# Layer 0's combining stage: gate, product and the first slots ahead of the preparation of attention's weights

## The chip, the cores and the metric

One core of a Trainium2 chip runs the whole program. The time is device microseconds of one execution; runs of one kernel are compared by their median. The engines are PE (TensorE), DVE (VectorE), ACT (ScalarE), POOL (GpSimd) and SP (SyncE, which issues DMAs).

## The reference, cut to what matters

A macaron block over 4096 tokens of width 256: half a mixture-of-experts layer, attention, half a mixture-of-experts layer, all in float32.

```python
def ffn(x, Wg, W1, W2, W3, Ws1, Ws2, Ws3):           # T = 4096, E = 32, TOP_K = 4
    weights, indices = top_k(softmax(x @ Wg), 4)
    y = zeros_like(x)
    for e in range(E):                                 # routed tokens of one expert
        y = y.at[tok].add(swiglu(x[tok], W1[e], W2[e], W3[e]) * w[:, None])
    return y + swiglu(x, Ws1, Ws2, Ws3)                # shared expert, for all tokens

def attn(x, qkv_w, qkv_b, proj_w, proj_b):             # 16 heads of width 16
    q, k, v = split(x @ qkv_w.T + qkv_b)
    return softmax(q @ k.T / sqrt(16)) @ v @ proj_w.T + proj_b

x = x + 0.5 * ffn(layernorm(x), ...)
x = x + attn(layernorm(x), ...)
x = x + 0.5 * ffn(layernorm(x), ...)                   # the same weights again
```

## The kernel before

The program runs in stages with a barrier between them: routing, experts, combining (`combine_project`), attention, and then routing, experts and combining again. The change is in `combine_project` alone, which runs once, at 387.9 to 608 us.

This stage handles 32 tiles of 128 tokens (`NT`), in 8 blocks of 4 (`TPB`). For each tile it fetches the four rows that the experts wrote for each token, one indirect DMA for each of the four (`pair_d` to `Y`), and adds them to `X` with their weights. It adds half of the shared expert's output, measures mean and variance, normalises, turns the block by matmuls with the identity, and multiplies by attention's weights to give q, k and v.

Before the tiles come two preparations. The first is the shared expert for block 0: `up` (matmuls into `psA` and `psB`), `gated` (Silu, ACT), `hidden` (gate times `psB`, DVE), for two halves `m`. The second is attention's weights: ACT squares four row blocks of `raw` and sums them, DVE's `balance_weights` works out powers of two from the sums (12 tiny operations) and scales the four row blocks, PE turns all eight row blocks through `psQ[0]` and `psQ[1]`, ACT copies them out, and v's bias is folded into `out_bias` (a matmul into `psV`, an addition on DVE).

The order on each engine is written out by hand, as a loop over slots `s` = 0 to 39. In slot `s` DVE adds tile `s` (`gathered`, four operations; `hidden` in odd slots; `shared`; `measured`), PE does a fourth of `up` for the next block and `down` for tile `s`, and from slot 7 on (`LAG`) PE also does `value` and `query_key` for a tile seven earlier. `down(t)` waits until DVE's `shared(t - 1)` has read `psZ`. At the last slot of a block DVE prepares the variance, in the slot behind it ACT takes the root and DVE normalises.

POOL issues the 128 gathers in a row, each with a small memset behind it (`pause`) that waits for the gather's issue. There are 16 slots in `Y`, so gather 17 (tile 4) waits for DVE's `gathered(0)`, and generally tile `t` for `gathered(t - 4)`; no weight of attention stands in that queue.

Of the kernel before, what the change touches and what calls it, by code (L numbers as in the profile page):

```python
# [28 lines left out]
HSC = HS // P  # L29
# [920 lines left out]
def combine_project(nc, a, f_sem, sb, pb, X, XNT, pair_d, pair_slot, pair_weight, ws1, ws3, ws2, ident, env):  # L950
# [6 lines left out]
    QB = 3  # L957
    LAG = TPB + 3
    SLOTS = NT + LAG + 1
    y_in = [env["sem"](f"y_in{s}") for s in range(YS)]  # L960
    sem = env["heads_sem"]
    V, ops, spare, norms = env["V"], env["ops"], env["spare"], env["norms"]
# [18 lines left out]
    with ExitStack() as c:  # L981
# [37 lines left out]
        with nc.Block() as block:  # L1019
# [66 lines left out]
            def _(pe):  # L1086
# [12 lines left out]
                def down(t):  # L1099
                    b, u = t // TPB, t % TPB  # L1100
                    if u == 0:
                        pe.wait_ge(f_sem("s_hid"), (b + 1) * HSC)
                    if t >= 1:
                        pe.wait_ge(f_sem("z_added"), t)
                    for m in range(HSC):
                        last = pe.matmul(psZ[:, :], hid[:, b % 2, m, u * P:(u + 1) * P], ws2[:, m, :],
                                         start=(m == 0), stop=(m == HSC - 1))
                    last.then_inc(f_sem("z_ready"), 1)

                def turn(b, pair):  # L1110
# [5 lines left out]
                            last = pe.transpose(psT[:, u, c, :], xn[:, 2 * pair + u, c * P:(c + 1) * P], ident[:, :])  # L1116
                    last.then_inc(sem("turned"), 1)

                def value(b, u):
                    t = b * TPB + u  # L1120
                    pe.wait_ge(sem("xnt_ready"), 2 * b + u // 2 + 1)
                    if t >= 1:
                        pe.wait_ge(sem("v_out"), t)
                    for c in range(DC):
                        last = pe.matmul(psV[:, :], xnt[:, c, u * P:(u + 1) * P], wt[:, c, 2 * D:],
                                         start=(c == 0), stop=(c == DC - 1))
                    last.then_inc(sem("v_in"), 1)
# [24 lines left out]
                pe.wait_ge(f_sem("ws"), 48)  # L1152
                for piece in range(2 * HSC):
                    up(0, piece)
                pe.wait_ge(sem("raw"), 32)
                for n, b in enumerate(ORDER):
                    if b < NE:
                        pe.wait_ge(sem("w_scaled"), b + 1)
                    if n >= 2:
                        pe.wait_ge(sem("w_out"), n - 1)  # L1160
                    for c in range(DC):
                        last = pe.transpose(psQ[n % 2][:, c * P:(c + 1) * P], raw[:, b, c * P:(c + 1) * P], ident[:, :])
                    last.then_inc(sem("w_turned"), 1)
                pe.wait_ge(sem("w_out"), NW)
                pe.wait_ge(sem("vwide"), 1)
                for c in range(DC):
                    last = pe.matmul(psV[:, :], vwide[:, c, :], pwt[:, c, :], start=(c == 0), stop=(c == DC - 1))
                last.then_inc(sem("vb_in"), 1)
                pe.wait_ge(sem("out_bias"), 1)
                pe.wait_ge(sem("heads"), 3)  # L1170
                for s in range(SLOTS):
                    now, past = projecting(s), projecting(s - TPB)
                    if s // TPB + 1 < NB:
                        up(s // TPB + 1, s % TPB)
                    if s < NT:
                        down(s)
                    if now is not None and now[1] == 0:
                        turn(now[0], 1)
                    if past is not None and past[1] == 0:
                        measure(past[0])  # L1180
# [14 lines left out]
            def _(act):  # L1195
                def gated(b, m):
                    act.wait_ge(f_sem("s_up"), b * 2 * HSC + 2 * m + 1)
                    if b * HSC + m >= 1:
                        act.wait_ge(f_sem("s_hid"), b * HSC + m)
                    act.activation(gate[:, :], psA[:, :], ACT.Silu).then_inc(f_sem("s_gate"), 1)  # L1200
# [19 lines left out]
                def squared(b, e):  # L1220
                    act.wait_ge(sem("high"), b * NE + e + 1)
                    act.activation(square[:, e, :], parts[:, e, 0, :], ACT.Square).then_inc(sem("squared"), 1)

                act.wait_ge(sem("raw"), 32)
                for e in range(NE):
                    act.activation(raw_sq, raw[:, e, :], ACT.Square, accum_out=square_sum[:, e:e + 1])\
                       .then_inc(sem("w_squared"), 1)
                    act.wait_ge(sem("w_squared"), e + 1)
                for m in range(HSC):
                    gated(0, m)  # L1230
                for n, b in enumerate(ORDER):
                    act.wait_ge(sem("w_turned"), n + 1)
                    dst = wt[:, :, b * P:(b + 1) * P] if b < NQ else pwt[:, :, (b - NQ) * P:(b - NQ + 1) * P]
                    act.activation(dst, psQ[n % 2][:, 0:D].rearrange("p (c q) -> p c q", c=DC), ACT.Copy).then_inc(sem("w_out"), 1)
                for s in range(SLOTS):
                    now, past = projecting(s), projecting(s - TPB)
                    if s % TPB == 0 and 1 <= s // TPB <= NB:
                        b = s // TPB - 1
                        act.wait_ge(sem("var"), b + 1)
                        act.activation(dev[:, b * TPB:(b + 1) * TPB], var[:, b * TPB:(b + 1) * TPB], ACT.Sqrt).then_inc(sem("dev"), 1)  # L1240
                    if now is not None and now[1] == 0:
                        turned(now[0], 1)
                    if past is not None and past[1] == 0:
                        b = past[0]
                        act.wait_ge(sem("norm_out"), 2 * b + 1)
                        if b == 0:
                            act.wait_ge(sem("steps_out"), 16 * 4)
                        act.activation(norms[:, b * BLK:(b + 1) * BLK], psQ[output(b, NE) % QB][0:NH, :], ACT.Copy)\
                           .then_inc(sem("norm_kept"), 1)
                    if s // TPB + 1 < NB and s % 2 == 0:  # L1250
                        gated(s // TPB + 1, s % TPB // 2)
                    if now is not None:
# [28 lines left out]
            def _(v):  # L1281
# [52 lines left out]
                    v.wait_ge(sem("norm_kept"), b + 1)  # L1334
                    v.sem_inc(sem("q_out"), 2)

                v.wait_ge(sem("bias"), 16)
                v.wait_ge(sem("w_squared"), NE)
                balance_weights(v, own.link, raw, bias, square_sum, span, expo_i, expo_f, power, sem("w_scaled"))
                v.wait_ge(sem("vbias"), 16)  # L1340
                v.tensor_copy(vwide, vbias[:, :].unsqueeze(2).to_broadcast([P, DC, P])).then_inc(sem("vwide"), 1)
                for m in range(HSC):
                    hidden(0, m)
                v.wait_ge(sem("pbias"), 16)
                v.wait_ge(sem("vb_in"), 1)
                v.tensor_tensor(out_bias[:, :], psV[:, :], out_bias[:, :], ALU.add).then_inc(sem("out_bias"), 1)
                for s in range(SLOTS):
                    now, past = projecting(s), projecting(s - TPB)
                    if s < NT:
                        gathered(s)  # L1350
                        if s % 2 == 1 and s // TPB + 1 < NB:
                            hidden(s // TPB + 1, s % TPB // 2)
                        shared(s)
                        measured(s)
                    if s < NT and s % TPB == TPB - 1:
# [461 lines left out]
```

## Time and profile before

| | us |
|---|---|
| median of 3 runs | 2913.71 (2913.23 to 2915.76) |
| the profiled execution | 2915.8 |
| its span | 2914.1 |
| busy in the span: PE, DVE, ACT, POOL | 2646.3, 2242.2, 2198.4, 715.6 |

The stage takes 220 of the 2914 us. Attention, which follows it, takes most of the span and is not touched. A row of a timeline reads: start, duration, engine, line, operation, what it writes <- what it reads, shapes, count, and in brackets how long the engine had been idle before it and what ended that. Rows in sequence of one line are merged. A float32 matmul of the program stands as two matmul instructions on PE.

### The profile page before, as it was taken

The page shows a single profiled execution, that of the slowest core. Times are in us where ns is not written, and L with a number is a line of the kernel's source. Part 1 is how long each engine was busy: PE and PEld are TensorE (multiplying, and loading weights), DVE is VectorE, ACT ScalarE, POOL GpSimd, SP SyncE. Part 2 cuts the span into 40 slices and gives each one's busy share as a digit, 9 for nine tenths or more (in the row PEclk, how much of TensorE's full clock was granted, in tenths as well). Part 3 has the DMA queues.
Part 4 walks back from the last instruction along what each step waited for, and adds up shares of the span by engine and source line. Part 5 has one row for each costly group of instructions (what it writes and reads, how often), then busy time and mean ns, then how long its engine had stood idle before and what let it go on. Part 6 is the DMA issues. An engine that isn't in the chain of part 4 may idle for free. (4 is left out here: it accounts for less than half of the span.)

```text
span 2914.1 us, 54682 instructions
## 1 busy us (share of the span) xinstructions
PE 2646.3 (91%) x17803; PEld 1087.4 (37%) x17803; DVE 2242.2 (77%) x4357; ACT 2198.4 (75%) x3178; POOL 715.6 (25%) x1002
## 2 busy tenths in 40 slices
PE   5799979959999999999999999999999984999971
PEld 5499845511222222122121222222222162999541
DVE  6777758858888888888888888888888767777454
ACT  4644425559999999999999999999999945444320
POOL 1566668730000000000000000000000014666576
PEclk9999999979999999999999999999999985999985
DMA  6555655520010010010010010010000026555644
GB/s 185 153 170 171 160 119 140 140 57 3 5 25 3 5 25 3 5 25 4 4 25 5 3 25 5 3 25 5 3 10 27 3 90 191 166 171 164 116 125 121
DMA packets 132280, 195.63 MB, mean 67 GB/s; under 512 B 22534, under 2 KB 99526, under 8 KB 130662
## 3 DMA queue, kind: packets, MB, share of 16 engines
q1 hardware_dynamic: 104208, 116.85, 14.3%
q0 software_dynamic: 27648, 75.53, 10.7%
q8 instruction: 146, 2.39, 0.4%
q14 instruction: 86, 0.70, 0.1%
q10 hardware_dynamic: 192, 0.15, 0.0%
HBM read 124.80 MB, written 67.50 MB: 66 GB/s over the span
## 5 line engine op out<-in xcount | busy, mean ns | idle before, releaser
L1686 ACT ACTIVATE RB<-psS 128x1024 f32<-128x1024 f32 x1856 | 1702.4, 1338 | 17.5 <-PE psS L1609 17.4
L1651 PE MATMUL psO<-RB,values 128*32 128x512 f32 x7424 | 991.8, 606 | 0.1
L1609 PE MATMUL psS<-WE 51*128 51x512 f16 x3712 | 667.4, 386 | 38.2 <-SPq L1574 8.1
L1609 PEld LDWEIGHTS psS<-WE 51*128 51x128 f16 x3712 | 165.1, 93 | 1034.7 <-ACT RB L1686 1013.0
L1707 DVE TENSOR_SCALAR scaled<-psO 128x512 int32<-128x512 f32 x384 | 265.0, 690 | 173.2 <-PE psO L1609 166.1
L660 POOL DMA_INDIRECT xg<-xn_d,index x320 | 305.3, 954 | 185.3 <-issue 152.1
L686 PE MATMUL psH<-xgt,chosen 128*128 128x128 f32 x2560 | 341.4, 277 | 0.0
L1568 POOL COPY values<-WE 128x464 f32<-128x464 f32 x12 | 6.8, 568 | 1266.4 <-PE psO L1651 1266.4
L686 PEld LDWEIGHTS psH<-xgt,chosen 128*128 128x128 f32 x2560 | 314.3, 193 | 0.6 <-issue 0.2
L773 ACT ACTIVATE gate<-psH 128x128 f32<-128x128 f32 x320 | 88.7, 277 | 261.5 <-PE psH L686 255.1
L1651 PEld LDWEIGHTS psO<-RB,values 128*32 128x32 f32 x7424 | 146.3, 108 | 308.1 <-issue 291.2
L695 PE MATMUL psO<-WE,hid 128*128 x640 | 191.0, 381 | 0.6 <-ACT ob L777 0.6
L749 DVE TENSOR_TENSOR hid<-gate,psH 128x128 f32<-128x128 f32 x320 | 92.0, 287 | 121.2 <-ACT gate L773 120.5
L777 ACT ACTIVATE ob<-psO 128x256 f32<-128x256 f32 x320 | 122.8, 384 | 52.6 <-PE psO L695 46.4
L736 DVE COPY chosen<-WE 128x512 f32 x320 | 134.9, 422 | 30.3 <-issue 27.9
L1609 PE MATMUL psO<-WE 51*128 51x512 f16 x384 | 145.6, 379 | 12.5 <-DVE scaled L1707 12.5
L676 PE MATMUL psX<-ident,xg 128*128 128x128 f32 x640 | 125.9, 279 | 22.2 <-DMA xg<-xn_d,index 21.0
L743 DVE COPY xgt<-psX 128x256 f32<-128x256 f32 x320 | 133.3, 417 | 13.3 <-PE psX L676 12.6
L1718 DVE TENSOR_SCALAR scaled<-scaled 128x1024 int32<-128x1024 int32 x192 | 135.9, 708 | 0.0
L1078 POOL DMA_INDIRECT WE<-pair_d,pair_slot x128 | 126.0, 985 | 24.7 <-issue 20.9
L1723 DVE SCALAR_TENSOR_TENSOR WE<-series 128x1024 f32<-128x1024 f32 x96 | 112.9, 1217 | 0.0
L1738 DVE SCALAR_TENSOR_TENSOR WE<-WE,scaled 128x1024 f32<-128x1024 f32 x96 | 112.9, 1217 | 0.0
(245 smaller groups left out, 3161.7 us busy)
## 6 DMA issues: line engine op xcount, KB each, us to landing
pair_d<-ob SPq DMA_DIRECT2D x320, 128.0 KB, 2.1
WE<-part_d SPq DMA_DIRECT2D x84, 128.0 KB
xn_d<-ws SPq DMA_DIRECT2D x64, 128.0 KB, 1.7
WE<-in_W SPq DMA_DIRECT2D x2, 4096.0 KB, 24.0
part_d<-raw SPq DMA_DIRECT2D x32, 256.0 KB, 3.0
xg<-xn_d,index POOLq DMA_INDIRECT x320
RA<-in_x SPq DMA_DIRECT2D x8, 512.0 KB, 7.3
head_d<-sums SPq DMA_DIRECT2D x128, 32.0 KB, 1.8
```

What stands on the lines that cost most here:

```text
L660: pool.indirect_dma_start(xg[:, u, :], None, xn_d, bass.IndirectOffsetOnAxis(ap=index[:, w, u:u + 1], axis=0))\
L676: last = pe.transpose(psX[j % 2][:, c * P:(c + 1) * P], xg[:, j % U, c * P:(c + 1) * P], ident[:, :])
L686: last = pe.matmul(psH[j % 2][:, n * P:(n + 1) * P], chosen[:, j % 2, c, n, :], xgt[:, j % 2, c * P:(c + 1) * P], start=(c == 0), stop=(c ...
L695: pe.matmul(psO[j % 2][:, :], hid[:, j % U, :], WE[:, e, DC * 2 * H:], start=True, stop=True).then_inc(sem("down"), 1)
L736: v.tensor_copy(chosen[:, j % 2, :, :, :].rearrange("p c n h -> p (c n h)"), WE[:, e, 0:DC * 2 * H])\
L743: v.tensor_copy(xgt[:, j % 2, :], psX[j % 2][:, :]).then_inc(sem("xgt_ready"), 1)
L1078: pool.indirect_dma_start(Y[:, s, :], None, pair_d, bass.IndirectOffsetOnAxis(ap=pair_slot[:, t, k:k + 1], axis=0))\
L1609: return pe.matmul(ps, K[r][rows, kt * P:(kt + 1) * P], Q[r][rows, first:first + BLK], start=True, stop=True)
L1651: last = pe.matmul(psO[g % 2][32 * j:32 * (j + 1), :], values[:, r, j % 2, kt, :], weights, start=(kt == 0), stop=(kt == order(g)[-1]))
L1686: act.activation(probs[m % RING], psS[m % HELD][:, :], ACT.Exp, scale=SCALE).then_inc(sem("exped"), 1)
L1707: v.tensor_scalar(scaled[at(g, u)][:, n * BLK:(n + 1) * BLK], bank[:, :], SCALE * LOG2E * 2 ** 23, LOWEST, ALU.mult, ALU.max).then_inc(sem ...
L1718: v.tensor_scalar(scaled[k], scaled[k], EXPONENT, FLIP, ALU.bitwise_and, ALU.bitwise_xor)\
```

## The change

`up(0, ...)` stays first on PE. Everything else of the weights' preparation moves back:

- ACT: `gated(0, 0)` and `gated(0, 1)` now stand ahead of the four squares; the eight copies out of `psQ` move into slot 3.
- DVE: `hidden(0, 0)`, `hidden(0, 1)` and slot 0 now stand ahead of `balance_weights` and the copy of v's bias; the addition to `out_bias` moves to slot 3, behind `measured(3)` and ahead of the variance.
- PE: the 16 transposes and the two matmuls of v's bias move to slot 3, behind `down(3)`. The wait for `out_bias` moves from slot 0 to the first `value`.

The instructions themselves, the DMAs and POOL's and SP's queues stay as they were.

```diff
+    WEIGHTS_AT = 3
 # PE
+                def weights():
+                    pe.wait_ge(sem("raw"), 32)
+                    for n, b in enumerate(ORDER):
+                        if b < NE:
+                            pe.wait_ge(sem("w_scaled"), b + 1)
+                        if n >= 2:
+                            pe.wait_ge(sem("w_out"), n - 1)
+                        for c in range(DC):
+                            last = pe.transpose(...)
+                        last.then_inc(sem("w_turned"), 1)
+                    pe.wait_ge(sem("w_out"), NW)
+                    pe.wait_ge(sem("vwide"), 1)
+                    ...                                # matmuls into psV
+                    last.then_inc(sem("vb_in"), 1)
 def value(b, u):
+                    if t == 0:
+                        pe.wait_ge(sem("out_bias"), 1)
...
                 for piece in range(2 * HSC):
                     up(0, piece)
-                pe.wait_ge(sem("raw"), 32)
-                ...                                    # the same as in weights()
-                pe.wait_ge(sem("out_bias"), 1)
                 pe.wait_ge(sem("heads"), 3)
                 for s in range(SLOTS):
...
                     if s < NT:
                         down(s)
+                    if s == WEIGHTS_AT:
+                        weights()
 # ACT
+                for m in range(HSC):
+                    gated(0, m)
                 act.wait_ge(sem("raw"), 32)
                 for e in range(NE):
                     act.activation(raw_sq, raw[:, e, :], ACT.Square, ...)
-                for m in range(HSC):
-                    gated(0, m)
-                for n, b in enumerate(ORDER):
-                    ...                                # eight copies
...
+                    if s == WEIGHTS_AT:
+                        for n, e in enumerate(ORDER):
+                            ...                        # the same eight copies
 # DVE
-                v.wait_ge(sem("bias"), 16)
-                v.wait_ge(sem("w_squared"), NE)
-                balance_weights(...)
-                v.wait_ge(sem("vbias"), 16)
-                v.tensor_copy(vwide, ...)
                 for m in range(HSC):
                     hidden(0, m)
-                v.wait_ge(sem("pbias"), 16)
-                v.wait_ge(sem("vb_in"), 1)
-                v.tensor_tensor(out_bias[:, :], psV[:, :], out_bias[:, :], ALU.add)
                 for s in range(SLOTS):
...
                         measured(s)
+                    if s == 0:
+                        ...                            # balance_weights and the copy, with their waits
+                    if s == WEIGHTS_AT:
+                        ...                            # the addition to out_bias, with its waits
```

On DVE at the stage's start, before (`span`, `expo` and `power` belong to `balance_weights`, `shid` is `hidden`, RA is `X`; L1341 is the copy of v's bias and L1346 the addition to `out_bias`):

```order
L945 TENSOR_TENSOR bias<-bias,power 128x4 [waits a_dve]
L947 TENSOR_SCALAR raw<-raw,power 128x256 [waits a_dve]
L947 TENSOR_SCALAR raw<-raw,power 128x256 x3
L1341 COPY axn<-vbias 128x256 [waits a_vbias]
L1287 TENSOR_TENSOR shid<-sgate,psB 128x512 [waits f0_s_up,f0_s_gate] x2
L1346 TENSOR_TENSOR WE<-psV,WE 128x256 [waits a_vb_in,a_pbias]
L1293 SCALAR_TENSOR_TENSOR RA<-WE,pair_weight,RA 128x256 [waits k_y_in0]
```

and there now:

```order
L1295 TENSOR_TENSOR shid<-sgate,psB 128x512 [waits f0_s_up,f0_s_gate] x2
L1301 SCALAR_TENSOR_TENSOR RA<-WE,pair_weight,RA 128x256 [waits k_y_in0]
L1301 SCALAR_TENSOR_TENSOR RA<-WE,pair_weight,RA 128x256 [waits k_y_in1,f0_y_used]
L1301 SCALAR_TENSOR_TENSOR RA<-WE,pair_weight,RA 128x256 [waits k_y_in2,f0_y_used]
L1301 SCALAR_TENSOR_TENSOR RA<-WE,pair_weight,RA 128x256 [waits k_y_in3,f0_y_used]
L1307 SCALAR_TENSOR_TENSOR RA<-psZ,RA 128x256 [waits f0_z_ready,f0_y_used]
L1312 BN_STATS astats<-RA 128x6 [waits f0_z_added]
L1314 BN_AGGR amv<-astats 128x2 [waits a_stats]
L934 TENSOR_TENSOR span<-bias 128x4 [waits a_w_squared,a_bias]
```

The four additions of tile 0, which release POOL's gather 17, moved from behind `out_bias` to a place behind the two `hidden`.

On PE, now, at the end of slot 3 (L1096 is `up`, L1107 `down`, L1128 the transposes, L1133 the matmuls of v's bias):

```order
L1107 MATMUL psZ0<-ws0,shid0 128x256 [waits f0_z_added]
L1107 MATMUL psZ0<-ws0,shid0 128x256
L1128 MATMUL psQ0<-ident,raw 128x128 [waits a_raw]
L1128 MATMUL psQ0<-ident,raw 128x128
L1128 MATMUL psQ1<-ident,raw 128x128 x2
L1128 MATMUL psQ0<-ident,raw 128x128 [waits a_w_out]
```

Before, the same 16 transposes stood between the last `up(0, ...)` and slot 0.

## Rows read from the trace of the kernel before

**Rows 1.** Page, costliest groups: the gathers' issue

```profile
L1078 POOL DMA_INDIRECT WE<-pair_d,pair_slot x128 | 126.0, 985 | 24.7 <-issue 20.9
```

**Rows 2.** Busy by stretch: us; PE, PEld, DVE, ACT, POOL; granted clock; DMA share, GB/s

```profile
387.90:411.70 23.80, 16.58 (x36) 6.90 (x36) 5.93 (x21) 5.86 (x18) 20.88 (x38) 0.71 0.56 150
411.70:426.40 14.70, 13.48 (x39) 7.24 (x40) 12.79 (x33) 2.48 (x3) 10.57 (x17) 1.00 0.28 78
488.30:556.40 68.10, 68.10 (x234) 40.55 (x233) 56.41 (x126) 37.24 (x67) 59.12 (x98) 1.00 0.58 153
```

**Rows 3.** Timeline of POOL at gathers 16 and 17, and at the last

```profile
410.50 0.95 POOL L1078 DMA_INDIRECT WE<-pair_d,pair_slot  x1 [0.17 <-issue]
414.51 0.95 POOL L1078 DMA_INDIRECT WE<-pair_d,pair_slot  x1 [2.83 <-DVE RA L1293]
...
568.07 0.95 POOL L1078 DMA_INDIRECT WE<-pair_d,pair_slot  x1 [0.17 <-issue]
```

**Rows 4.** Line L1078: durations in ns, starts, its waits (us, times), landing

```profile
L1078 POOL DMA_INDIRECT WE<-pair_d,pair_slot x128: 951/952/1216, 390.3 to 568.1; - x128
...
  DVE RA L1293: 3.8, 7
...
DMA to landing us min/median/max: 2.7/2.9/5.6
```

**Rows 5.** Timeline from the stage's start to slot 0

```profile
387.95 2.67 PE L1095 MATMUL psA<-RB,ws 128*128 128x512 f32 x4 [3.65 <-PEq L647]
390.41 2.90 PE L1095 MATMUL psB<-RB,ws 128*128 128x512 f32 x4
...
397.06 0.60 ACT L1200 ACTIVATE sgate<-psA 128x512 f32<-128x512 f32 x1
397.14 0.16 DVE L934 TENSOR_TENSOR span<-bias 128x4 f32<-128x4 f32 x1 [14.00 <-ACT axn L1226]
397.71 3.78 PE L1095 MATMUL psA<-RB,ws 128*128 128x512 f32 x4 [4.40 <-ACT sgate L1200]
401.75 0.67 DVE L1287 TENSOR_TENSOR shid<-sgate,psB 128x512 f32<-128x512 f32 x1
406.05 0.64 PE L1162 MATMUL psQ<-ident,raw 128*128 128x128 f32 x4
411.32 0.42 DVE L1346 TENSOR_TENSOR WE<-psV,WE 128x256 f32<-128x256 f32 x1 [4.28 <-PE psV L1167]
411.66 2.04 DVE L1293 SCALAR_TENSOR_TENSOR RA<-WE,pair_weight,RA 128x256 f32<-128x256 f32 x4
411.80 1.98 PE L1095 MATMUL psA<-RB,ws 128*128 128x512 f32 x4 [0.59 <-DVE WE L1346]
```

**Rows 6.** Timeline of DVE, `gathered` of slots 1 and 4

```profile
415.78 2.01 DVE L1293 SCALAR_TENSOR_TENSOR RA<-WE,pair_weight,RA 128x256 f32<-128x256 f32 x4
426.37 2.04 DVE L1293 SCALAR_TENSOR_TENSOR RA<-WE,pair_weight,RA 128x256 f32<-128x256 f32 x4
```

**Rows 7.** Busy time by stretch again: shorter stretches around the pause of PE

```profile
392.75:393.60 0.85, 0.56 (x2) 0.00 (x0) 0.00 (x0) 0.00 (x0) 0.68 (x2) 1.00 0.89 142
396.15:405.50 9.35, 6.81 (x8) 2.58 (x9) 4.86 (x18) 2.04 (x6) 8.20 (x15) 0.50 0.57 138
```

**Rows 8.** Timeline, slot 9: its last gather, DVE's reading, PE's next `down`

```profile
446.31 0.95 POOL L1078 DMA_INDIRECT WE<-pair_d,pair_slot  x1 [0.16 <-issue]
451.66 0.43 DVE L1304 BATCH_NORM_STATS2 astats<-RA 128x6 f32<-128x256 f32 x1
453.27 1.03 PE L1106 MATMUL psZ<-ws,shid 128*128 128x256 f32 x4
```

**Rows 9.** Timeline, slot 31 and what follows it

```profile
569.91 2.04 DVE L1293 SCALAR_TENSOR_TENSOR RA<-WE,pair_weight,RA 128x256 f32<-128x256 f32 x4
573.91 0.59 ACT L1248 ACTIVATE WE<-psQ 16x512 bf16<-16x512 f32 x1 [2.38 <-DVE query_norm L1331]
574.90 1.10 PE L1125 MATMUL psV<-wt,axnt 128*128 128x256 f32 x4 [0.27 <-ACT WE L1255]
```

More of the change, by code:

```diff
@@ L1117, in turn @@
                     last.then_inc(sem("turned"), 1)
+                def weights():
[6 more added lines that the diff above has]
+                        for c in range(DC):
+                            last = pe.transpose(psQ[n % 2][:, c * P:(c + 1) * P], raw[:, b, c * P:(c + 1) * P], ident[:, :])
+                        last.then_inc(sem("w_turned"), 1)
+                    pe.wait_ge(sem("w_out"), NW)
+                    pe.wait_ge(sem("vwide"), 1)
+                    for c in range(DC):
+                        last = pe.matmul(psV[:, :], vwide[:, c, :], pwt[:, c, :], start=(c == 0), stop=(c == DC - 1))
+                    last.then_inc(sem("vb_in"), 1)
                 def value(b, u):
                     t = b * TPB + u
+                    if t == 0:
+                        pe.wait_ge(sem("out_bias"), 1)
                     pe.wait_ge(sem("xnt_ready"), 2 * b + u // 2 + 1)
@@ L1154, in _ @@
                     up(0, piece)
-                pe.wait_ge(sem("raw"), 32)
-                for n, b in enumerate(ORDER):
[L1157 to L1168, printed above, removed]
-                pe.wait_ge(sem("out_bias"), 1)
                 pe.wait_ge(sem("heads"), 3)
@@ L1228, in _ @@
                     act.wait_ge(sem("w_squared"), e + 1)
-                for m in range(HSC):
-                    gated(0, m)
[L1231 to L1234, printed above, removed]
                 for s in range(SLOTS):
@@ L1251, in _ @@
                         gated(s // TPB + 1, s % TPB // 2)
+                    if s == WEIGHTS_AT:
+                        for n, e in enumerate(ORDER):
+                            act.wait_ge(sem("w_turned"), n + 1)
+                            dst = wt[:, :, e * P:(e + 1) * P] if e < NQ else pwt[:, :, (e - NQ) * P:(e - NQ + 1) * P]
+                            act.activation(dst, psQ[n % 2][:, 0:D].rearrange("p (c q) -> p c q", c=DC), ACT.Copy)\
+                               .then_inc(sem("w_out"), 1)
                     if now is not None:
@@ L1335, in longest @@
                     v.sem_inc(sem("q_out"), 2)
-                v.wait_ge(sem("bias"), 16)
-                v.wait_ge(sem("w_squared"), NE)
-                balance_weights(v, own.link, raw, bias, square_sum, span, expo_i, expo_f, power, sem("w_scaled"))
-                v.wait_ge(sem("vbias"), 16)
-                v.tensor_copy(vwide, vbias[:, :].unsqueeze(2).to_broadcast([P, DC, P])).then_inc(sem("vwide"), 1)
                 for m in range(HSC):
                     hidden(0, m)
-                v.wait_ge(sem("pbias"), 16)
-                v.wait_ge(sem("vb_in"), 1)
-                v.tensor_tensor(out_bias[:, :], psV[:, :], out_bias[:, :], ALU.add).then_inc(sem("out_bias"), 1)
                 for s in range(SLOTS):
@@ L1354, in _ @@
                         measured(s)
+                    if s == 0:
+                        v.wait_ge(sem("bias"), 16)
+                        v.wait_ge(sem("w_squared"), NE)
+                        balance_weights(v, own.link, raw, bias, square_sum, span, expo_i, expo_f, power, sem("w_scaled"))
+                        v.wait_ge(sem("vbias"), 16)
+                        v.tensor_copy(vwide, vbias[:, :].unsqueeze(2).to_broadcast([P, DC, P])).then_inc(sem("vwide"), 1)
+                    if s == WEIGHTS_AT:
+                        v.wait_ge(sem("pbias"), 16)
+                        v.wait_ge(sem("vb_in"), 1)
+                        v.tensor_tensor(out_bias[:, :], psV[:, :], out_bias[:, :], ALU.add).then_inc(sem("out_bias"), 1)
                     if s < NT and s % TPB == TPB - 1:
```

## The prediction, made before the changed kernel had run

> **What bounds the kernel now.** I read the busy time by stretch first, then POOL's timeline, then the timeline from the stage's start to slot 0, and last the place where the gathers end.
>
> From 488.3 to 556.4 us PE is busy for all of its 68.10 us, at the full clock [rows 2]. So in the slots that project (from slot 7 to about 27) PE sets the pace, and work that reaches PE earlier there ends earlier. Ahead of that it does not: in the 14.7 us of slots 0 to 3 DVE is busy for 12.79 us, and in the 23.8 us before slot 0 PE only for 16.58 [rows 2].
>
> POOL is the second chain. It issues 128 gathers in a row, 985 ns each [rows 1]. The first starts at 390.3 [rows 4], the sixteenth at 410.50 [rows 3]: 15 periods of 1.35 us, never waiting. Gather 17 could start at 410.50 + 1.35 = 411.85. It starts at 414.51, since it waited 2.83 us for DVE's additions of tile 0 [rows 3]. From there to the last at 568.07 [rows 3] are 111 periods of 1.383 us; of the whole stage's waits for DVE, 3.8 us in 7 [rows 4], the 2.83 are the one that is longer than POOL's usual pause of 0.17.
>
> The two chains meet at the end. The last gather is issued at 568.07 and, with the median landing of 2.9 us [rows 4], is there at 570.97. Slot 31 needs it for its fourth addition, at 569.91 + 3 x 0.51 = 571.44 [rows 9] (a quarter of 2.04 us is 0.51). That is a slack of 0.47 us. And slot 31 is on the path: what DVE does at its end releases ACT at 573.91, and PE's `value` at 574.90 waits 0.27 us for ACT's next copy [rows 9]. Behind that stand only the last projections, the shift's rows and the barrier.
>
> **The change part by part.**
>
> *The start of slot 0.* The first `psA` is complete at 387.95 + 2.67 = 390.62, the first `psB` at 390.41 + 2.90 = 393.31 [rows 5]. ACT's gate no longer has the squares ahead of it, so it runs at about 390.8 to 391.4 (0.60 us [rows 5]), and DVE's first `hidden` at 393.5 to 394.2 (0.67 us [rows 5]), not at 401.75. PE's pause of 4.40 us before 397.71 goes [rows 5]. PE issues its third piece at about 393.0 and has two to do. What one costs depends on the clock: 3.78 us at the granted clock of 0.50, 1.98 at 1.00 [rows 5, 7]; chained pieces overlap a little. The clock was at 1.00 (2.4 GHz) in 392.75 to 393.60, the stretch in which PE ran out of work; after the pause it was down at 0.50 (1.2 GHz) from 396.15 to 405.50 [rows 7]. The first `psB` at 2.90 us lies between the two durations, so the clock had come up during it. With work at hand I expect it to stay up: the two pieces end near 396.6, `hidden(0, 1)` at 397.5, and slot 0 starts there, 14.2 us before its 411.66 [rows 5]. At half clock it would be 393.0 + 2 x 3.78 + 0.9, about 401.4. Its four rows were issued by 390.3 + 3 x 1.35 and have landed at 397.3, or at 400 with the longest landing of 5.6 us [rows 4].
>
> *Gather 17.* Tile 0 is added by 397.5 + 2.04 = 399.5, or 404 in the worse case, both ahead of 411.85. So POOL's wait goes and every later gather can be issued 414.51 - 411.85 = 2.66 us earlier. No later one is held by DVE: tile 5 would ask for tile 1 at 411.85 + 5.5 = 417.4, and tile 1 is added by about 408.5.
>
> *What slots 0 to 3 take up.* Before, they lasted 426.37 - 411.66 = 14.71 us [rows 5, 6]. Now `balance_weights` and the copy stand in slot 0: from 397.14 to 401.75, 4.61 us of DVE [rows 5], all of it on DVE's path, because DVE is the engine that is nearly full there. In slot 3 DVE waits for PE and ACT: from the first transpose to `out_bias` are 411.32 - 406.05 = 5.27 us, and 0.34 more until the next operation [rows 5]. About 1.1 us of this lies beside `shared(3)` and `measured(3)` (estimated from the 0.43 us of the operation between them [rows 8], three short operations), so 4.5 us are added. Slot 4 starts at 397.5 + 14.7 + 4.6 + 4.5 = 421.3, against 426.37 [rows 6]: 5.1 us earlier. The squares move into ACT's idle time (5.86 us busy of 23.8 [rows 2]) and cost nothing; they are ready long before DVE asks for them. The eight copies on ACT are counted in the 5.27 us. Moving the wait for `out_bias` costs nothing: the first `value` is in slot 7.
>
> The bounds of this term: with PE at half clock all along, slot 0 starts at 401.4 and the 5.27 us of transposes, which ran at full clock, at most double. That gives 421.3 + 3.9 + 5.3 = 430.5, 4.1 us later than before. The best case is the 5.1 us, and perhaps 1 us more, since slot 0 waited about 1 us for its `psZ`, which PE now has ready. I take 5.1: every term but the clock has its own row.
>
> Here the trace and a rule have to be held against each other. The pause of 4.4 us before 397.71 was followed by a granted clock of 0.50 [rows 5, 7]. The change makes a new pause: PE has nothing to do between `down(1)`, done near 403.5, and `down(2)`, which waits for `shared(1)`. That comes at 397.5 + 4.1 (slot 0 [rows 5, 6]) + 4.6 + 3.1 = 409.3. PE is idle for 5.8 us, longer than the pause that cost the clock before. So `down(2)`, `up(1, 3)` and perhaps `down(3)` run at half clock: 1.8 us for the `up` (3.78 against 1.98 [rows 5]) and about 0.9 for a `down` (an estimate, nearly the 1.03 us of one at full clock again [rows 8]), of which DVE's own 3 to 3.7 us per slot cover most. Slot 4 could then be at 424.0, 2.4 us earlier than before instead of 5.1. The Trainium skill says the same in its page "TensorE: Matmul & The Clock Gate", section "Why this matters for your kernels": a long enough idle gap between bursts of matmuls puts the clock back to half rate. By that rule this change trades one fall of the clock for another; the trace of before agrees as far as it goes.
>
> *What is late next.* From slot 7 on PE is full, and an earlier start is kept, but the gathers came forward by 2.66 us only. The tightest place ahead of the end is slot 9. Its last gather is issued at 446.31, lands at 449.2, and needs an addition, `hidden` and `shared` (0.51 + 0.67 + 0.42 and about 0.2 of gaps = 1.8 us) until `shared(9)` ends at 451.0 at the earliest. It ended about 451.6 (the next operation starts at 451.66), and `down(10)` started at 453.27 [rows 8], 2.3 us after 451.0. So PE can be at most 2.66 + 2.3 = 4.9 us earlier from here on. At slot 31 the slack is 0.47 us: its last addition can be at most 2.66 + 0.47 = 3.1 us earlier, and the rest of the stage, then attention and the second layer, follow with that.
>
> *Sum.* 3.1 us of the 5.1 arrive. The profiled execution took 2915.8 us, so 2912.7. It lies 2.1 above the median of 2913.7, and so does the changed one: 2910.6 us by median.
>
> One size is unsure from both sides: the 111 later periods are 0.036 us longer than the first 15 (single issues take up to 1216 ns [rows 4]), 4.0 us in all. What does this is not shown. The DVE work beside the later gathers is the same as before, so I leave it. If it vanished, POOL could gain 6.7 and PE's 4.9 would decide; if it doubled, the stage would be 0.9 us longer than before.
>
> **The rivals.**
>
> - *PE's gain arrives whole.* The gathers of the last slots are held up less, and POOL does not bind at slot 31. The time falls by 4.9 us to 2908.8. For it: single delays of 0.2 us decide here, and landing varies from 2.7 us. Against it: a slack of 0.47 us at slot 31, and no reason why POOL's periods should shorten.
> - *Slots 0 to 3 eat the gain.* The clock falls in the new pause and DVE, which has 4.6 us more to do in slot 0, is late: slot 4 comes 0 to 2 us earlier. DVE and PE are then behind POOL, whose gain lies idle. 1 us: 2912.7. For it: DVE's 12.79 of 14.7 us [rows 2] and the row on the clock.
> - *Slower, through slot 3.* The transposes are serial between PE and ACT, and DVE stands behind them in slot 3 with tile 4 and all later ones queued behind it. If they run at half clock, slot 4 starts at 424.0 + 5.3 = 429.3, 2.9 us later than before, and PE, which is full from slot 7 on, keeps it to the end: 2916.6. It decides as soon as slot 4 starts later than 426.37. Against it: `up(1, 3)` and `down(3)` run just ahead of the transposes, as a burst did in [rows 7] before the clock rose.
> - *Something that I have no term for*, such as attention starting at another moment relative to POOL's and DVE's first work there, 6 us or more to either side.
>
> **How the numbers follow.** POOL sets the gain: 0.56. PE's gain whole: 0.13. Eaten in slots 0 to 3: 0.18. Slower through slot 3: 0.06. No term: 0.07. The time is that of the first, 2910.6. The range of 8 in 10 reaches from a little below the second rival, with a microsecond for the spread of runs (2913.23 to 2915.76), to the neighbourhood of no change: 2907.2 to 2914.6. A measurement of this kernel tells about 0.2% (5.8 us) from no change; the forecast and all the worked rivals are smaller. Faster by more than that needs nearly the best case of slot 4 and no POOL limit, or the last rival: 0.10. Slower: half of the last rival and a bit of the fourth: 0.05. Within: 0.85.
>
> **What the changed profile would show.** Slot 0's additions start near 397.5 and gather 17 near 411.85 with no wait for DVE. The clock stays at 1.00 from 392.75 on and falls near slot 2. `out_bias` starts near 420.5, slot 4 near 421.3. In slots 8 to 11 and at slot 31 DVE waits for gathers, where before its additions ran through (2.04 us for four). The last gather is issued near 565.4 and slot 31's fourth addition at 568.3. I am wrong if gather 17 still waits, if slot 4 comes after 423.3 (then slots 0 to 3 set the gain), or if the shift at slot 31 is not the shift at the end.

## The result, and the profile after

The changed kernel took 2909.03 us (median of 20 runs), the kernel before 2913.74 (20 runs); the ratio is 0.9986, with a 95% interval of 0.9979 to 0.9992. The ratio is of fast runs alone and leaves out two of the 20 runs of the kernel before, at 6204 and 8001 us. By the ratio that is 4.1 us less (2.3 to 6.1 by the interval), a little under what I had called measurable. The forecast was 2910.6.

The profiled execution has a span of 2904.1 us, 10.0 less than the one before. 3.3 us of that lie in the stage: from its first `up` matmul to attention's first matmul are 613.44 - 387.95 = 225.5 us before and 608.45 - 386.22 = 222.2 after. Another 1.7 us (387.95 - 386.22) were there before the stage began, where no code was changed, 1.0 lies in attention and about 4 behind it. Of another execution of the same kernel (the third group of experiments) the span was 2908.6 us and the stage 221.8, and attention took 1719.3 us, as before the change, not 1718.2: the stage repeats within 0.4 us, the rest wanders by some microseconds. Below, times are therefore counted from the stage's first `up`, before from 387.95, after from 386.22.

The first view is the timeline of PE and DVE over the stage's start (start, duration, engine, line, operation, operands, shapes, count, idle time before and what ended it).

```profile
386.22 3.75 PE L1096 MATMUL psA<-RB,ws 128*128 128x512 f32 x4 [3.59 <-PEq L647]
389.76 2.61 PE L1096 MATMUL psB<-RB,ws 128*128 128x512 f32 x4
392.21 1.88 PE L1096 MATMUL psA<-RB,ws 128*128 128x512 f32 x4
393.93 1.88 PE L1096 MATMUL psB<-RB,ws 128*128 128x512 f32 x4
...
395.92 0.69 DVE L1295 TENSOR_TENSOR shid<-sgate,psB 128x512 f32<-128x512 f32 x1 [2.74 <-PE psB L1096]
396.52 2.10 DVE L1301 SCALAR_TENSOR_TENSOR RA<-WE,pair_weight,RA 128x256 f32<-128x256 f32 x4
...
407.22 2.08 PE L1107 MATMUL psZ<-ws,shid 128*128 128x256 f32 x4 [4.53 <-DVE RA L1307]
409.08 3.19 PE L1096 MATMUL psB<-RB,ws 128*128 128x512 f32 x4
...
418.20 0.42 DVE L1364 TENSOR_TENSOR WE<-psV,WE 128x256 f32<-128x256 f32 x1 [3.63 <-PE psV L1133]
418.61 2.04 DVE L1301 SCALAR_TENSOR_TENSOR RA<-WE,pair_weight,RA 128x256 f32<-128x256 f32 x4
```

PE's four pieces now run in one burst, and slot 0's additions start 10.30 us into the stage rather than 23.71 [rows 5]. Slots 0 to 3 then take 22.1 us rather than 14.7, and slot 4 starts at 32.4 us rather than 38.4 [rows 6]: 6.0 of the 13.4 us are left. In the middle PE stands idle for 4.53 us before `down(2)`, which waits for `shared(1)`, and the matmuls behind the pause are slow: `down(2)` takes 2.08 us and the `up` behind it 3.19, where a `down` takes 1.03 [rows 8] and an `up` 1.88 (above).

The busy time by stretch (us; PE, PEld, DVE, ACT, POOL; granted clock; DMA share, GB/s) shows the clock there:

```profile
386.20:396.50 10.30, 10.28 (x18) 4.46 (x19) 1.27 (x2) 2.87 (x9) 8.99 (x18) 0.76 0.75 200
396.50:418.60 22.10, 16.26 (x53) 9.50 (x52) 17.21 (x50) 5.36 (x13) 19.35 (x33) 0.85 0.38 104
392.00:400.00 8.00, 8.00 (x22) 3.86 (x21) 4.53 (x11) 3.12 (x10) 7.01 (x13) 1.00 0.69 167
405.00:411.00 6.00, 3.78 (x7) 2.40 (x8) 5.61 (x15) 0.60 (x1) 5.34 (x9) 0.50 0.35 96
412.00:420.00 8.00, 6.69 (x31) 4.22 (x30) 4.16 (x11) 5.17 (x11) 7.00 (x13) 1.00 0.35 98
486.60:554.70 68.10, 67.33 (x228) 39.37 (x227) 56.49 (x127) 36.93 (x68) 59.12 (x99) 1.00 0.59 153
```

It is at 1.00 from 392 us on, in the second half of the burst, at 0.50 behind the pause and at 1.00 again for the transposes. DVE is busy for 5.61 of the 6.00 us at half clock: it loses next to nothing to the slow `down(2)` there; what it loses later, because the transposes start later, the third group of experiments tells. The last row is PE's full stretch, which was 68.10 us of 68.10 in [rows 2].

POOL's timeline at gathers 16 and 17, and line L1079's summary (durations in ns, start of the first and of the last gather; its waits; who waited for it):

```profile
408.95 1.12 POOL L1079 DMA_INDIRECT WE<-pair_d,pair_slot  x1 [0.17 <-DVE RA L1301]
...
410.46 0.95 POOL L1079 DMA_INDIRECT WE<-pair_d,pair_slot  x1 [0.17 <-issue]
...
L1079 POOL DMA_INDIRECT WE<-pair_d,pair_slot x128: 951/952/1201, 388.6 to 563.3; - x128
...
  DVE RA L1301: 1.5, 9
who waited for it (us, times):
  DVE RA L1301: 6.7, 7
```

Gather 17 has lost its wait of 2.83 us [rows 3] and is issued at 24.24 us, 2.3 earlier. The last is 3.08 earlier (177.04 us instead of 180.12). But DVE now waits for gathers, 6.7 us in 7 times. Here are three of those waits, and the place where PE is held for the last time:

```profile
431.52 0.49 DVE L1301 SCALAR_TENSOR_TENSOR RA<-WE,pair_weight,RA 128x256 f32<-128x256 f32 x1 [1.00 <-DMA WE<-pair_d,pair_slot]
...
439.67 0.48 DVE L1301 SCALAR_TENSOR_TENSOR RA<-WE,pair_weight,RA 128x256 f32<-128x256 f32 x1 [1.46 <-DMA WE<-pair_d,pair_slot]
...
452.90 0.95 POOL L1079 DMA_INDIRECT WE<-pair_d,pair_slot  x1 [0.17 <-issue]
...
456.91 0.48 DVE L1301 SCALAR_TENSOR_TENSOR RA<-WE,pair_weight,RA 128x256 f32<-128x256 f32 x1 [1.96 <-DMA WE<-pair_d,pair_slot]
...
471.04 1.13 PE L1107 MATMUL psZ<-ws,shid 128*128 128x256 f32 x4 [0.40 <-DVE RA L1307]
```

Measured at `measured` of each slot, slots 1 to 3 are 10.0 us earlier than before, 4 to 6 are 5.9, 7 is 3.5, 8 and 9 are 2.5, 10 is 3.1, 11 is 1.55 and 12 to 14 are 1.6 to 2.0; from slot 15 on it is 3.08 without a change to slot 31. Line L1312 of after and line L1304 of before, over slots 15 to 31 (first and last start), show the two ends of that:

```profile
L1312 DVE BATCH_NORM_STATS2 astats<-RA x17: 426/427/428, 479.6 to 567.6; 128x6 f32<-128x256 f32 x17
```

```profile
L1304 DVE BATCH_NORM_STATS2 astats<-RA x17: 427/427/428, 484.4 to 572.4; 128x6 f32<-128x256 f32 x17
```

4.8 us at either end, of which 1.7 are older than the stage.

The kernel before had one such wait already, which the prediction passed over: the last gather of slot 10 was issued at 451.78 and used at 455.22, 3.44 us later, and DVE waited for it.

```profile
451.78 0.95 POOL L1078 DMA_INDIRECT WE<-pair_d,pair_slot  x1 [0.17 <-issue]
...
455.22 0.48 DVE L1293 SCALAR_TENSOR_TENSOR RA<-WE,pair_weight,RA 128x256 f32<-128x256 f32 x1 [0.23 <-DMA WE<-pair_d,pair_slot]
```

### The profile page after: what moved, and what is told of

Its sections match the earlier page's. It is cut to its first block and busy times, and to the rows that moved or that the text cites. A ratio compares the mean times of both kernels' runs of the same rounds, so it can differ in the third digit from the quotient of the medians.

```text
span 2904.1 us, 54674 instructions
## 1 busy us (share of the span) xinstructions
PE 2641.0 (91%) x17801; PEld 1086.2 (37%) x17803; DVE 2241.1 (77%) x4357; ACT 2198.1 (76%) x3178; POOL 713.5 (25%) x1002
## 3 DMA queue, kind: packets, MB, share of 16 engines
q0 software_dynamic: 27648, 75.53, 10.8%
## 5 line engine op out<-in xcount | busy, mean ns | idle before, releaser
L743 DVE COPY xgt<-psX 128x256 f32<-128x256 f32 x320 | 133.4, 417 | 11.2 <-PE psX L676 11.0
L1079 POOL DMA_INDIRECT WE<-pair_d,pair_slot x128 | 125.6, 982 | 22.0 <-issue 20.6
L1738 DVE SCALAR_TENSOR_TENSOR series<-WE 128x1024 f32<-128x1024 f32 x96 | 112.8, 1216 | 0.0
```

What stands on the lines that cost most here:

```text
L743: v.tensor_copy(xgt[:, j % 2, :], psX[j % 2][:, :]).then_inc(sem("xgt_ready"), 1)
L1079: pool.indirect_dma_start(Y[:, s, :], None, pair_d, bass.IndirectOffsetOnAxis(ap=pair_slot[:, t, k:k + 1], axis=0))\
```

## The experiments

Stage lengths, from the first `up` to attention's first matmul. The changed kernel is "after". They ran in three groups of four; the kernels of a group shared a chip and the runs of before, against which each ratio is taken. The parts of the stage are read from one execution of each kernel.

### First group: a condition in which the stage took 50 us more

While this group ran the kernels before and after took about 3055 us (before: 3054.53), on the same chip on which the next group took 2911; it is compared within itself only.

After, unchanged:

> The changed kernel once more, so that the others have it on the same chip. The stage (first matmul of L1096 to the first of attention, L1619) took 225.5 us before and 222.2 after. Both theories: 222.2 again, within 0.3. If attention's own start (1.1 us shorter in the trace of after) belongs to the change, its first stretch is as short here; if it is luck of the clock at that moment, it differs from run to run.

3055.89 us, ratio 0.9998 (0.9986 to 1.001); the stage took 275.8 us.

After, with a shorter pause ahead of each gather:

```diff
-                        pool.memset(pause[:, 0:P], 0.0).then_inc(f_sem("paused"), 1)
+                        pool.memset(pause[:, 0:16], 0.0).then_inc(f_sem("paused"), 1)
```

> The changed kernel with POOL's memset behind each gather cut from 128 to 16 columns (0.22 us to perhaps 0.1): POOL's 128 gathers end some 14 us earlier, PE and DVE as they are. Theory POOL (gathers limit the gain): DVE no longer waits for gathers in slots 7 to 11, slot 4's gain of 6.0 us (relative to the stage's start) reaches slot 15 and the end, and the stage takes 219.5 (2.7 less than after). Rival PE (the 3.1 us are all that slots 0 to 3 give, the gathers are a side effect): 222.2 as after. Rival contention (faster gathers and their transfers hold up DVE or the stores): longer than 222.2.

3062.92 us, 1.0027 (1.0011 to 1.0042), stage 282.2.

Before, with the same edit:

> The kernel before with the same shorter memset. Theory POOL: before the change PE was the limit (slot 10 waited 0.2 us for a gather), so nothing or up to 0.3 us comes of it: 225.3 us for the stage. Rival PE: the same, 225.5. If the gathers had been the limit before as well, up to 3 us less.

3074.01 us, 1.006 (1.0042 to 1.0079), stage 296.0.

After, with gather 17 held until tile 3 is added, so that POOL's gain is taken back and nothing else:

```diff
-                    pool.wait_ge(f_sem("y_used"), (t + 1) * TOPK)
+                    pool.wait_ge(f_sem("y_used"), (t + 1) * TOPK if t != 4 else YS + 4 * TOPK)
```

> The changed kernel, but gather 17 waits for tile 3's additions instead of tile 0's, so that it starts about 2.6 us later, relative to the stage's start nearly where it was before (26.8 against 26.6 us), while PE's and DVE's order stays that of after. Theory POOL: the gain goes with it, the stage takes 224.9 to 225.5. Rival PE: 222.2 to 222.6, as after.

3057.28 us, 1.0005 (0.9993 to 1.0017), stage 277.9.

None of the four answers the question, because something else bound the stage. The summary of the gathers' line in the first of them, and a stretch of 260 us of it:

```profile
L1079 POOL DMA_INDIRECT WE<-pair_d,pair_slot x128: 952/955/1197, 418.1 to 628.9; - x128
...
  DVE RA L1301: 37.8, 10
...
420.00:680.00 260.00, 202.01 (x626) 111.09 (x624) 157.16 (x362) 100.59 (x190) 151.21 (x254) 0.92 0.39 106
```

POOL waits for DVE's additions for 37.8 us, not for 1.5, and PE was busy for 78% of the stretch. But DVE's additions did not wait for rows: nothing waited for a gather in this trace. What DVE waited for is seen in slot 2:

```profile
440.01 2.07 PE L1107 MATMUL psZ<-ws,shid 128*128 128x256 f32 x4 [7.78 <-issue]
...
440.55 2.01 DVE L1301 SCALAR_TENSOR_TENSOR RA<-WE,pair_weight,RA 128x256 f32<-128x256 f32 x4
...
453.77 0.43 DVE L1307 SCALAR_TENSOR_TENSOR RA<-psZ,RA 128x256 f32<-128x256 f32 x1 [11.20 <-remote]
```

The four additions run through in 2.01 us, and then `shared(2)` stands for 11.20 us ahead of `psZ`, although the matmuls of `down(2)` had started at 440.01. ACT's first copy out of `psQ` likewise starts at 464.33, where the transposes that it waits for had started at 456.11. POOL, through the 16 buffers, waits behind DVE. So in these places it is the hand-over from PE to DVE and ACT that is late, and the gathers only follow. With the shorter pause the stage was 6.4 us longer still (282.2 against 275.8). Under that condition the change is worth nothing (0.9998). Why the hand-over is late I could not find in these traces.

### Second group: which chain caps the gain (before: 2911.53)

**Gate and product first, weights left where they were.** Before, with ACT's gates ahead of the squares and DVE's `hidden` ahead of balancing, but scaling, transposes and bias folding still ahead of slot 0:

```diff
+                for m in range(HSC):
+                    gated(0, m)
                 act.wait_ge(sem("raw"), 32)
...
-                for m in range(HSC):
-                    gated(0, m)
...
+                for m in range(HSC):
+                    hidden(0, m)
                 v.wait_ge(sem("bias"), 16)
...
-                for m in range(HSC):
-                    hidden(0, m)
```

> The kernel before with one part of the change: ACT's two gates ahead of the squares, DVE's two products ahead of the balancing; the weights' preparation stays ahead of slot 0. Where the chip lands gathers as in the traces of before and after (stage 225.5 and 222.2 us): slot 0's additions start about 17.4 us after the stage's start, not 23.8, and gather 17 starts without a wait. Theory POOL: the same cap as in after, 222.2 to 222.6 us, although nothing was moved into slots. Rival (the gain needs the weights in the slots): 223.5 to 225.5.

2909.87 us, 0.9994 (0.9985 to 1.0003), stage 224.4. Slot 0 started at 19.0 us, not 17.4, and slots 1 to 7 are 2.8 us earlier than before, the later ones 1.1. POOL came forward by 2.6 us, but its gain lay idle: DVE waited for no gather. PE's timeline shows where the rest went:

```profile
400.99 0.72 PE L1162 MATMUL psQ<-ident,raw 128*128 128x128 f32 x4 [2.05 <-DVE raw L947]
...
405.81 3.78 PE L1095 MATMUL psA<-RB,ws 128*128 128x512 f32 x4 [0.59 <-DVE WE L1346]
...
430.08 1.89 PE L1106 MATMUL psZ<-ws,shid 128*128 128x256 f32 x4 [2.32 <-DVE RA L1299]
```

PE idles in short pieces through the transposes, and the `up` behind them takes 3.78 us: half clock. It happens again at 430, behind a pause of 2.32 us; there the 2.8 us shrink to 1.1. The stage lies in the range of the rival, not of theory POOL: in this execution an early start of PE and POOL alone did not give what the change gives, and the two falls of the clock took about 3.6 us of it (slot 0 is 4.7 us earlier, slots 1 to 7 are 2.8, the later ones 1.1). Whether it would without them was not tried.

**The shorter pause on after**, by the same edit as in the first group.

> As e1_after_short_pause, whose chip took 50 us more for this stage whatever the kernel, so that it could not tell. On a chip as in before and after: theory POOL 219.5 us for the stage and no waits for gathers in slots 7 to 11; rival PE 222.2; rival contention more than 222.2. On a chip like that of e1, gathers' landing sets the stage and denser gathers cost 5 us or more again.

2905.9 us, 0.9979 (0.997 to 0.9988), stage 221.3, where theory POOL had 219.5; no DMA wait of DVE is left, and slots 4 to 30 are 5.9 us earlier than before. So the pace of POOL's gathers was what took the gain from 5.9 to 3.1 in slots 7 to 15. Then 1.9 us were lost at the very end. PE's timeline in slot 30 and two stretches:

```profile
557.08 1.13 PE L1107 MATMUL psZ<-ws,shid 128*128 128x256 f32 x4 [1.98 <-DVE RA L1307]
...
559.35 3.13 PE L1158 MATMUL psQ<-axnt,wt 128*128 128x512 f32 x4
...
540.00:557.00 17.00, 14.31 (x52) 8.26 (x50) 14.07 (x31) 9.52 (x18) 11.07 (x20) 1.00 0.47 132
558.50:561.50 3.00, 3.00 (x6) 1.66 (x5) 2.79 (x7) 0.38 (x1) 0.00 (x0) 0.50 0.26 87
```

In the last slots there is no `up` left for PE; it pauses for DVE, and behind a pause of 1.98 us the clock is down at 0.50 and the projection takes 3.13 us instead of 1.88.

**The shorter pause on before.**

> As e2_before_short_pause. Theory POOL: before the change the gathers were no limit, 225.3 us for the stage; rival contention: longer than 225.5, as on the other chip (20 us longer there).

2911.35 us, 0.9998 (0.9989 to 1.0007), stage 224.1 (expected 225.3). All slots, slot 0 too, are 1.4 to 1.5 us earlier, so denser gathers did not do it: slot 0's additions wait for PE's and ACT's work, not for rows. PE's timeline ahead of slot 0:

```profile
389.95 2.89 PE L1095 MATMUL psB<-RB,ws 128*128 128x512 f32 x4
396.25 3.78 PE L1095 MATMUL psA<-RB,ws 128*128 128x512 f32 x4 [3.41 <-ACT sgate L1200]
400.30 2.91 PE L1095 MATMUL psB<-RB,ws 128*128 128x512 f32 x4 [0.27 <-DVE shid L1287]
```

The last of these took 2.91 us: the clock rose during it. In the execution of before, the same piece began after an idle time of 0.98 us and took 3.78. So the 1.4 us (225.5 and 224.1) go with the moment at which the clock rises, and before gains nothing from denser gathers: its POOL waits for DVE at gather 17 anyway.

**Gather 17 held.**

> As e3_after_held_17. Theory POOL: with gather 17 back where it was relative to the stage's start (26.8 us), the stage takes 224.9 to 225.5 us though PE and DVE are as early as in after. Rival PE: 222.2 to 222.6.

2910.28 us, 0.9996 (0.9987 to 1.0005), stage 224.5, 0.4 less than theory POOL had and 1.9 more than the rival. POOL's timeline and the summary of its line:

```profile
412.44 0.95 POOL L1079 DMA_INDIRECT WE<-pair_d,pair_slot  x1 [3.01 <-DVE RA L1301]
...
  DVE RA L1301: 11.3, 14
DMA to landing us min/median/max: 2.7/2.9/5.3
```

Slots 1 to 4 are at least as early as in after (11.2 to 6.0 us earlier than before, 10.0 to 5.9 in after); but gather 17 stands at 27.15 us into the stage, DVE waits for gathers for 11.3 us in 14 times (6.7 in 7 in after), and the slots end 0.8 us earlier than before, not 3.1. With PE's and DVE's gain whole and POOL's alone taken back, three quarters of the gain are gone. This is the experiment that decides, together with the shorter pause on after, which relieves POOL and gives more. It does so by the traces: the intervals of the ratios, 0.9987 to 1.0005 here and 0.9979 to 0.9992 for the change, overlap.

### Third group: what keeping the clock is worth (before: 2912.77)

**After, once more.**

> The changed kernel again, beside its variants. In the trace: stage 222.2 us within 0.5, gather 17 24.2 us after the stage's start, DVE waits for gathers between slots 7 and 11.

2909.28 us, 0.9987 (0.9978 to 0.9996), stage 221.8. DVE waits for gathers 7.7 us in 8 times, all but 1.3 us of it in slots 7 to 11. The slots end 3.45 us earlier than before.

**Fillers in PE's new pause, pause of POOL as in after.** Five matmuls of the right length, into a PSUM tile that is free there; their results go nowhere:

```diff
                         up(s // TPB + 1, s % TPB)
+                    for _ in range({2: 5}.get(s, 0)):
+                        pe.matmul((psQ[2] if s < 4 else psA)[:, :], ws1[:, 0, 0:P], XNT[:, 0, 0, :], start=True, stop=True)
```

> The changed kernel with POOL's full memset and the same five matmuls ahead of down(2). Theory POOL: slot 4 is 7.7 us earlier than before, but the gathers cap the gain as before: DVE waits longer for them in slots 7 to 11, the stage takes 222.0 to 222.3. Rival PE (slots 0 to 3 set the gain in the changed kernel): 220.4.

2908.15 us, 0.9983 (0.9974 to 0.9992), stage 221.6 (theory POOL 222.0 to 222.3, rival 220.4). PE's fillers and two of DVE's later waits:

```profile
403.76 4.45 PE L1180 MATMUL psQ<-RB,ws 128*128 128x512 f32 x10
408.39 1.13 PE L1107 MATMUL psZ<-ws,shid 128*128 128x256 f32 x4 [0.17 <-DVE RA L1309]
...
452.53 0.48 DVE L1303 SCALAR_TENSOR_TENSOR RA<-WE,pair_weight,RA 128x256 f32<-128x256 f32 x1 [2.13 <-DMA WE<-pair_d,pair_slot]
...
479.98 0.48 DVE L1303 SCALAR_TENSOR_TENSOR RA<-WE,pair_weight,RA 128x256 f32<-128x256 f32 x1 [2.18 <-DMA WE<-pair_d,pair_slot]
```

`down(2)` takes 1.13 us, not 2.08, and slot 4 is 7.5 us earlier than before, not 5.9. At the end 3.7 are left, against 3.1 and 3.4 in the two executions of after: of the extra 1.5 us the most turn into waits for gathers, 9.0 us in all.

**Fillers and the shorter pause together.**

> f1 (the changed kernel, POOL's memset 16 columns wide) with five matmuls of 512 columns on PE in the pause ahead of down(2), into an unused part of psQ, results unused. In f1 the clock fell there, and slot 4 came 6.0 us earlier than before although DVE lost nothing in slots 1 to 3; the transposes came late instead. Theory clock (the fall costs about 1.8 us ahead of the transposes, and with POOL out of the way this reaches the end): the granted clock stays at 1.00 to slot 4, slot 4 is 7.7 us earlier than before, the stage takes 219.5 us (f1: 221.3). Rival (the transposes' end is set by ACT or DVE): 221.3.

2903.94 us, 0.9968 (0.9956 to 0.998): 8.8 us less than before by the medians, and, with the next one, the fastest version. The stage took 218.2 us (expected 219.5). Slot 4's additions, and the stretches that answer to those above:

```profile
417.94 2.04 DVE L1303 SCALAR_TENSOR_TENSOR RA<-WE,pair_weight,RA 128x256 f32<-128x256 f32 x4
...
394.00:411.00 17.00, 16.91 (x46) 8.12 (x44) 13.29 (x39) 3.71 (x11) 14.53 (x29) 1.00 0.46 127
558.50:561.50 3.00, 2.92 (x12) 1.56 (x10) 2.82 (x7) 1.63 (x5) 0.00 (x0) 1.00 0.26 87
```

The stage began at 386.96, so slot 4 starts 31.0 us into it, and the 7.2 us that the slots gain there arrive nearly whole at slot 31 (7.1). The clock also stayed up at the end, which no edit had touched; a fall there had cost 1.9 us in the run without fillers.

What the fall of the clock costs is best read from the length of slots 0 to 3, since slot 0 itself starts at 9.5 to 10.8 us into the stage, by the moment of the clock's first rise. They take 22.0 to 22.1 us in the three runs where the clock falls in that pause (after, after once more, the shorter pause alone) and 20.2 to 20.3 in the three with fillers: 1.8 us.

**The same, with fillers in slots 29 and 30 too** (`{2: 5, 29: 1, 30: 2}`).

> g1 with three more such matmuls, one in slot 29 and two in slot 30, in PE's pauses ahead of down. In f1 the clock fell at slot 30 (matmuls of value and query_key at half) and slot 31 was 4.0 us earlier than before where slot 30 was 5.7. Theory clock: no fall, stage 217.7 us, about 2.6 us less than f1 in all. Rival (the fall comes from the pauses in sum, or the matmuls delay down): 219.5 or more.

2904.07 us, 0.997 (0.9959 to 0.9981), stage 218.1 (expected 217.7). The clock did not fall, but nor had it in the run without the three, so nothing could come of them. The gathers bind again here: slot 0 started early, at 9.51 us, slots 4 to 6 were 8.5 us earlier than before, and DVE then waited for gathers for 5.0 us in 6 times, 2.21 of them for slot 11's last; 7.2 us were left. So even with the shorter pause late rows cap the gain, at 7.2 us here instead of 3.1 to 3.7.

## Why the prediction was right, and where it was not

*The start of slot 0: right.* Forecast 9.55 us into the stage, measured 10.30. The 0.75 us are the clock's: the first `psA` and `psB` took 3.75 and 2.61 us, where [rows 5] have 2.67 and 2.90, since it rose later.

*Gather 17: right.* Forecast at 23.9 us with no wait, measured at 24.24 with its usual 0.17.

*What slots 0 to 3 take up: nearly right.* Forecast 9.1 us more without a fall of the clock, measured 7.4 with one (22.1 against 14.7). The work on the weights in slot 0 took 404.08 - 399.67 = 4.4 us (4.6 forecast); in slot 3, from `measured` to slot 4, 4.0 (4.5 forecast). The other 1 us is the one that I had named and left out, slot 0's own wait for `psZ`. So slot 4 came 6.0 us earlier, not 5.1. This nearness is in part luck. With the clock kept up by fillers slots 0 to 3 took only 5.5 us more than before, and from `measured(3)` to slot 4 were 2.3 us: the transposes then start 0.4 us behind DVE's first addition of tile 3, so that 3.3 us of the 5.27 lie beside DVE's own work, where the working had counted 1.1. The term was 3.6 us too large for the case that it describes, and the fall of the clock, which the sum left out, took half of that.

*The clock: right in place, small in price.* It fell in the new pause as forecast: 4.53 us idle, and then 0.50. The Trainium skill has the same in "TensorE: Matmul & The Clock Gate", section "Why this matters for your kernels", and the trace agrees. The experiments with fillers in that pause put the price at 1.8 us at slot 4, where the rival had up to 2.7, and at 0.2 to 0.6 us at the end as long as POOL caps.

*What is late next: the right engine, the wrong place.* The step that failed is "At slot 31 the slack is 0.47 us". The forecast let PE run 4.9 us ahead through slot 9 and cut it back to 3.1 at slot 31. Measured, PE's `down` is 5.9 us earlier than before at slots 6 and 7; the rows that are late in slots 7 and 8 cut that to 4.0 by slot 11, and those of slot 11 to 3.08 by slot 15; after that nothing waits for a gather. The working counted a landing of 2.9 us, the median, for a last gather. Slot 11's was issued at 452.90 and used at 456.91, after 4.0 us, and then DVE ran through slots 11 to 13 with one more idle time, of 0.9 us (for ACT, which had itself waited for DVE), until `shared(13)` let `down(14)` go at 471.04. So the last 0.9 us of the cut go back to a single gather, 1.1 us later than the median, because the time that PE loses there, at full load, never comes back. It is no single event: slot 11's last gather was used 3.7 to 4.2 us after its issue, with a wait, in three other runs too, and where it was not (the fillers alone) slot 15's was, after 4.2.

At slot 31 no gather was late at all: the last came 3.08 us earlier, not 2.66, just as far as DVE and PE. Gather 17 was 2.3 us earlier (2.66 forecast), and the 111 periods behind it had come down from 1.383 to 1.377 us, 0.76 us in all. What makes these periods longer, which the prediction left open, the traces show. Over the 111 the issues take 4.05 us more than 0.952 us each before, and 3.32 us more after; all the rest is 149.5 us both times. And 25 of the 26 issues of before that took over 1 us, and all 23 of after, lie beside one of DVE's additions (of the 102 others of before 43 do). Why there are fewer of them after is not shown.

So 3.1 us forecast and 3.3 measured in the stage have the same cause, a row of gathers that could only come 2.3 to 3.1 us forward, but their nearness is partly luck: the place and the size of the slack were wrong, and the total came out. The rival "PE's gain arrives whole" needed the shorter pause as well; there it measured 5.9 us at slots 4 to 30. "Slots 0 to 3 eat the gain" is refuted by slot 4, and "slower, through slot 3" too: the transposes ran at full clock. The medians differ by 4.7 us, 1.4 more than the stage; that the rest is chance between runs is within the interval, not shown.

## What to carry to other kernels

Where two chains alternate, work out for each how far it can come forward, and expect the smaller; and take for the meeting point the latest arrivals on the way, not the median at the end. A gain that lies idle (3.8 of 7.5 us with the fillers alone) is had by relieving the other chain: a shorter pause between gathers did nothing for the kernel before, and on top of the change and the fillers it took 3.4 us off the stage (221.6 to 218.2). Where a new order leaves the matmul engine a pause, look at the clock behind it, and fill the pause only if nothing else caps the gain.

## What the runs showed of the hardware

- In the last slots PE is busy for 14.31 of 17.00 us in one run and 14.40 in another, with pauses of 1.98 and 1.78 us; in the first the clock fell to 0.50 and cost 1.9 us, in the second it stayed at 1.00. Where that decides was not found.
- The moment of the clock's first rise differs between executions of one kernel: the first two pieces of the changed kernel took 3.75 and 2.61 us in one and 2.90 and 2.67 in another, and slot 0 started at 10.30 and 9.51 us into the stage. Between before and its variant with the shorter pause it made 1.4 us.
- Gather issues take 0.95 us, but up to 1.2 beside DVE's additions (two inputs of 128x256 and one output, float32): 25 of the 26 over 1 us before and 23 of 23 after stood beside one, but so did 43 of the 102 shorter ones of before.
- The landing of the same gather differs: slot 11's last was used 4.01 us after its issue in one run and 2.93 in another with DVE waiting both times, where the median landing is 2.9 to 3.0.
- The 16 transposes of 128x128 in the loose burst from 412 to 420 us (PE busy for 6.69 of 8.00) ran at a granted clock of 1.00.
- A chip can be slower in such a stage for a while: the changed kernel took 3056 us on the chip on which its two variants later took 2906 and 2910, with a stage of 275.8 us and attention as ever (1718.2). DVE then waited for 11.20 us on a result of PE whose matmuls had started ahead of the wait, and for no gather. What does this was not found.
